# Projections of a transformer layer done as three bf16 products of split operands in place of fp32 products

## The reference

```python
def attn(x, Wq, Wkv_down, Wk_up, Wv_up, Wout):        # 16 heads of 64
    q = einsum('bld,dhk->blhk', x, Wq)
    latent = einsum('bld,dc->blc', x, Wkv_down)
    k = einsum('blc,chk->blhk', latent, Wk_up)
    v = einsum('blc,chk->blhk', latent, Wv_up)
    a = softmax(causal_mask(einsum('bqhd,bkhd->bhqk', q, k) / sqrt(64)))
    return einsum('bqhd,hdo->bqo', einsum('bhqk,bkhd->bqhd', a, v), Wout)

def ffn(x, Wg, bg, We, be):
    logits = x @ Wg + bg
    best_p = max over the 8 of softmax(logits)
    return (x @ We + be) * best_p[:, None]

x = x + layernorm(attn(layernorm(x), ...))
x = x + layernorm(ffn(layernorm(x), ...))
```

## Time and profile before

| | |
|---|---|
| time before, median of 2 runs | 2663.24 us (2646.28 to 2680.2) |
| the profiled execution | 2671.72 us |
| its span, slowest core (core 2) | 2670.2 us |
| spans of the eight cores | 2643.7 to 2670.2 us |
| TensorE matmul busy | 2046.2 us, 77% |
| ScalarE busy | 599.7 us, 22% |
| VectorE busy | 567.9 us, 21% |

### The profile page before, as it was taken

How to read it: one execution, slowest core, us unless ns; L and a number is a source line. 1 busy time by engine, 2 the same in 40 slices (tenths; PEclk the granted TensorE clock), 3 DMA queues, 4 the chain that set the end, 5 groups by cost and what they waited for, 6 DMA issues and landing times.

```text
span 2670.2 us, 18908 instructions; the slowest of 8 cores (2643.7 to 2670.2 us)
## 1 busy us (share of the span) xinstructions
PE 2046.2 (77%) x5377; PEld 786.7 (29%) x5377; DVE 567.9 (21%) x1050; ACT 599.7 (22%) x1372; POOL 75.4 (3%) x148
## 2 busy tenths in 40 slices
PE   5998987688696896877958769679699734458886
PEld 2444442122221222222222222122244322224443
DVE  2001001311312113122131121221000254323333
ACT  1111010044241442423414325134000111100000
POOL 0000000000000000000000000000000000000000
PEclk9777877799798897988979879789799866669998
DMA  3222210022121211211212212121200011002222
GB/s 91 71 71 79 63 49 27 4 9 8 8 8 8 8 6 8 10 9 11 14 12 16 16 26 16 10 11 14 32 16 24 17 40 47 24 16 95 89 93 71
DMA packets 101089, 83.31 MB, mean 31 GB/s; under 512 B 5248, under 2 KB 91776, under 8 KB 100992
## 3 DMA queue, kind: packets, MB, share of 16 engines
q0 software_dynamic: 11520, 37.76, 12.9%
q1 hardware_dynamic: 89472, 44.35, 6.0%
HBM read 61.12 MB, written 8.39 MB: 26 GB/s over the span
## 4 chain that ended last, share of the span: by engine, by line
PE 66%; DVE 12%; DMA 9%; issue 7%; ACT 5%; DVEq 1%; ACTq 0%; POOLq 0%; POOL 0%; SPq 0%
PE p L250 21%; PE p L488 14%; PE p L719 8%; PE p L432 8%; DMA PS<-SCR 7%; PE p L349 3%; PE p L363 2%; PE p L209 2%; DVE EB L478 1%; PE p L316 1%; ACT DSCR L472 1%; PE p L642 1%; ACT SCR L513 1%; ACT EB L458 1%; DVE EB L613 1%
## 5 line engine op out<-in xcount | busy, mean ns | idle before, releaser
L488 PE MATMUL p<-EB,VB 128*65 128x512 f32 (+3 forms) x1280 | 556.5, 553 | 120.6 <-DVE EB L478 102.3
L250 PE MATMUL p<-A,WS 128*128 128x512 f32 x1152 | 566.6, 661 | 28.8 <-DMA A<-PS 24.2
L250 PEld LDWEIGHTS p<-A,WS 128*128 128x128 f32 x1152 | 242.8, 211 | 349.6 <-issue 349.6
L432 PE MATMUL p<-B,KP 64*128 64x512 f32 (+3 forms) x640 | 319.7, 589 | 0.0
L437 PE MATMUL p<-B,KP 64*128 64x512 f32 (+3 forms) x640 | 319.6, 589 | 0.0
L458 ACT ACTIVATE EB<-p,NEGB 128x512 f32<-128x512 f32 x384 | 240.5, 685 | 255.7 <-PE p L437 255.1
L488 PEld LDWEIGHTS p<-EB,VB 128*65 128x65 f32 x1280 | 146.7, 139 | 482.2 <-issue 478.2
L719 PE MATMUL p<-B,WS 128*128 128x512 f32 x512 | 225.3, 603 | 0.0
L349 PE MATMUL p<-C,WU 128*128 128x512 f32 x256 | 128.6, 661 | 93.7 <-DVE KP L357 93.7
L432 PEld LDWEIGHTS p<-B,KP 64*128 64x128 f32 x640 | 101.0, 192 | 231.7 <-issue 231.7
L478 DVE TENSOR_TENSOR EB<-DSCR,TRI 128x128 f32<-128x128 f32 x256 | 74.7, 292 | 347.0 <-ACT DSCR L472 319.9
(11 more groups left out here) (92 smaller groups left out, 1069.3 us busy)
## 6 DMA issues: line engine op xcount, KB each, us to landing
XT<-x POOLq DMA_DIRECT2D x32, 512.0 KB, 3.9
WS<-wq SPq DMA_DIRECT2D x32, 512.0 KB, 4.5
WS<-we SPq DMA_DIRECT2D x32, 512.0 KB, 3.8
PS<-SCR POOLq DMA_DIRECT2D x64, 128.0 KB, 6.2
y<-XT POOLq DMA_DIRECT2D x16, 512.0 KB, 2.9
WS<-wkv SPq DMA_DIRECT2D x8, 512.0 KB, 4.4
A<-PS POOLq DMA_DIRECT2D x32, 128.0 KB, 2.2
WS<-wout SPq DMA_DIRECT2D x8, 512.0 KB, 3.9
```

What stands on the lines that cost most here:

```text
L250: r = o.matmul(ps[bank][:], WS[:, wslot * 1024 + kc * 128: wslot * 1024 + kc * 128 + 128], rhs_of(kc, nb), start=(kc == 0), stop=(kc == kc ...
L432: o.matmul(pA_[:, q0:512], KP[0:64, kc * 128:(kc + 1) * 128], B[0:64, p * 2048 + qb * 512 + q0: p * 2048 + (qb + 1) * 512], start=True, st ...
L488: return o.matmul(ps[pvbank][0:65, q0:512], VB[:, kc * 130 + sl * 65: kc * 130 + sl * 65 + 65], EB[:, eoff + q0:eoff + 512], start=(kc == ...
```

## The change

The products of `p2_part`, the output projection and the expert product are done in bf16. Each operand is written as hi + lo, where hi is its bf16 rounding and lo is the bf16 rounding of the rest, and each fp32 product becomes three bf16 products into the same PSUM bank: hi x hi, hi x lo and lo x hi. The up-projections, scores, value products, gate and transposes stay in fp32.

- **Weights** are split once (`wsplit`): load 128 columns over SP, ScalarE copies them to a bf16 hi, VectorE subtracts to a bf16 lo, and two DMAs on POOL's queue write both to internal DRAM tensors. The ten slices of wkv and wq are done at the very start, all landing in C under the one buffer `bC`. The slices of wout and we are done one each at the head of every pair of the attention, both landing in the same half of XT and both using the same half of the bf16 view of WS. All write-backs name one buffer, `bWH`.
- **Weights are read back** (`stream_b16`) by two DMAs of 256 KB each (128 runs of 2 KB) for every block of products, over SP.
- **Activations** are split before each 512-token stretch (`act_split`): eight ScalarE copies into AHI and eight VectorE subtractions into ALO. AHI lies over EB and ALO over VB; each exists once.
- **The output projection** has its loops turned: stretches outside, weight blocks inside, with 64 loads (32 pairs) in place of 8.
- The memset of VB is dropped, with its two columns of ones set after the q norms; the gate's weight goes to a tile of its own; `p6_b` normalizes through PS1 in place of EB.

```diff
+    AHI = nc.alloc_sbuf_tensor_at("AHI", [128, 4096], BF16, offset=nc.lookup_mloc(EB).addr)
+    ALO = nc.alloc_sbuf_tensor_at("ALO", [128, 4096], BF16, offset=nc.lookup_mloc(VB).addr)
+    WSB = nc.alloc_sbuf_tensor_at("WSB", [128, 4096], BF16, offset=nc.lookup_mloc(WS).addr)
+    bSTG = bEB + [bVB]
+    bWH = Buf("WHD")
-    s.op("vector", lambda o: o.memset(VB[:], 0.0), writes=[bVB])
+    def wsplit(dsrc, dhid, dlod, m, land, landbuf):
+        src = dsrc[:, m * 128:(m + 1) * 128].rearrange("(c p) n -> p c n",
+                                                       p=128)
+        landr = land.rearrange("p (c n) -> p c n", n=128)
+        s.op("sync", dma(landr, src), writes=[landbuf])
+        slot = m % 2
+        hi = WSB[:, slot * 2048:slot * 2048 + 1024]
+        lo = WSB[:, slot * 2048 + 1024:slot * 2048 + 2048]
+        s.op("scalar", lambda o, hi=hi, land=land: o.copy(hi, land),
+             reads=[landbuf], writes=[bWS[slot]])
+        s.op("vector", lambda o, hi=hi, lo=lo, land=land: o.tensor_sub(
+            lo, land, hi), reads=[landbuf, bWS[slot]], writes=[bWS[slot]])
+        s.op("gpsimd", dma(dhid[:, m * 1024:(m + 1) * 1024], hi),
+             reads=[bWS[slot]], writes=[bWH])
+        s.op("gpsimd", dma(dlod[:, m * 1024:(m + 1) * 1024], lo),
+             reads=[bWS[slot]], writes=[bWH])
+    for m in range(2):
+        wsplit(d_wkv, d_wkvh, d_wkvl, m, C[...], bC)
+    for m in range(8):
+        wsplit(d_wq, d_wqh, d_wql, m, C[...], bC)
...
+    def act_split(src_of, srcbufs, kchunks=8):
+        for kc in range(kchunks):
+            s.op("scalar", lambda o, kc=kc: o.copy(
+                AHI[:, kc * 512:(kc + 1) * 512], src_of(kc)),
+                reads=srcbufs, writes=[bSTG[kc % 5]])
+            s.op("vector", lambda o, kc=kc: o.tensor_sub(
+                ALO[:, kc * 512:(kc + 1) * 512], src_of(kc),
+                AHI[:, kc * 512:(kc + 1) * 512]),
+                reads=srcbufs + [bSTG[kc % 5]], writes=[bSTG[(kc + 1) % 5]])
+    def proj3(dst, dstbufs, wslot, kchunks, bank, scale=None, evac=None):
...
+                r = o.matmul(ps[bank][:], hw_, ha_, start=(kc == 0), stop=False)
+                r = o.matmul(ps[bank][:], hw_, la_, start=False, stop=False)
+                r = o.matmul(ps[bank][:], lw_, ha_, start=False,
+                             stop=(kc == kchunks - 1))
...
+        s.op("tensor", mmg, reads=[bWS[wslot]] + bSTG, writes=[bP[bank]])
+    def stream_b16(dhid, dlod, m, slot):
+        s.op("sync", dma(WSB[:, slot * 2048:slot * 2048 + 1024],
+                         dhid[:, m * 1024:(m + 1) * 1024]),
+             reads=[bWH], writes=[bWS[slot]])
+        s.op("sync", dma(WSB[:, slot * 2048 + 1024:slot * 2048 + 2048],
+                         dlod[:, m * 1024:(m + 1) * 1024]),
+             reads=[bWH], writes=[bWS[slot]])
     def p2_part(nb):
+        act_split(lambda kc, nb=nb: lnT_of(kc, nb), bAs[4 * nb:4 * nb + 4])
         for m in range(2):
...
+            stream_b16(d_wkvh, d_wkvl, m, slot)
+            proj3(C[...], [bC], slot, 8, 4 + m % 4)
...
     for p in range(8):
+        wsplit(d_wout, d_wouth, d_woutl, p, XT[... p % 2 ...], bXT[p % 2])
+        wsplit(d_we, d_weh, d_wel, p, XT[... p % 2 ...], bXT[p % 2])
         for wi, dsrc in enumerate((d_wku, d_wvu)):
...
+    for nb in range(4):
+        act_split(lambda kc, nb=nb: oT_of(kc, nb), list(bAs))
+        for m in range(8):
+            stream_b16(d_wouth, d_woutl, m, slot)
+            proj3(B[...], bBs[4 * nb:4 * nb + 4], slot, 8, (m + 2) % 4)
...
     for s4 in range(4):
+        act_split(lambda kc, s4=s4: ln3_of(kc, s4), bBs[4 * s4:4 * s4 + 4])
         for mf in range(8):
+            stream_b16(d_weh, d_wel, mf, slot)
...
+            proj3(None, None, slot, 8, bank, evac=ev)
```

More of the change, by code:

```diff
@@ L138, in build_nc @@
     DSCR = sb("DSCR", 256)
+    WGS = sb("WGS", 64)
     QN = KNS = DRS = LG = BPROW = SCR
+    AHI = nc.alloc_sbuf_tensor_at("AHI", [128, 4096], BF16,
+                                  offset=nc.lookup_mloc(EB).addr)
+    ALO = nc.alloc_sbuf_tensor_at("ALO", [128, 4096], BF16,
+                                  offset=nc.lookup_mloc(VB).addr)
+    WSB = nc.alloc_sbuf_tensor_at("WSB", [128, 4096], BF16,
+                                  offset=nc.lookup_mloc(WS).addr)
     ps = [es.enter_context(nc.psum_tensor(f"p{i}", [128, 512], F32))
@@ new lines, in proj3, with mmg @@
+    def proj3(dst, dstbufs, wslot, kchunks, bank, scale=None,
+              evac=None):
+        def mmg(o, wslot=wslot, kchunks=kchunks, bank=bank):
+            n = 0
+            for kc in range(kchunks):
+                hw_ = WSB[:, wslot * 2048 + kc * 128:
+                          wslot * 2048 + kc * 128 + 128]
+                lw_ = WSB[:, wslot * 2048 + 1024 + kc * 128:
+                          wslot * 2048 + 1024 + kc * 128 + 128]
+                ha_ = AHI[:, kc * 512:(kc + 1) * 512]
+                la_ = ALO[:, kc * 512:(kc + 1) * 512]
+                r = o.matmul(ps[bank][:], hw_, ha_, start=(kc == 0),
+                             stop=False)
+                r = o.matmul(ps[bank][:], hw_, la_, start=False, stop=False)
+                r = o.matmul(ps[bank][:], lw_, ha_, start=False,
+                             stop=(kc == kchunks - 1))
+            return r
+        s.op("tensor", mmg, reads=[bWS[wslot]] + bSTG, writes=[bP[bank]])
+        if evac is not None:
+            evac(bank)
+        elif scale is None:
+            s.op("scalar", lambda o, bank=bank: o.copy(
+                dst, ps[bank][:]), reads=[bP[bank]], writes=dstbufs)
+        else:
+            s.op("scalar", lambda o, bank=bank: o.activation(
+                dst, ps[bank][:], AF.Copy, scale=scale),
+                reads=[bP[bank]], writes=dstbufs)
@@ L290, in p2_part @@
+            proj3(C[:, m * 2048 + nb * 512:m * 2048 + nb * 512 + 512],
+                  [bC], slot, 8, 4 + m % 4)
         for m in range(8):
             slot = m % 2
[L292 to L301, removed]
+            stream_b16(d_wqh, d_wql, m, slot)
@@ L332, in build_nc @@
          reads=[bP[7]], writes=[bROWS])
+    s.op("vector", lambda o: o.memset(vb3[:, :, 64:65], 1.0), writes=[bVB])
+    s.op("vector", lambda o: o.memset(vb3[:, :, 129:130], 1.0), writes=[bVB])
     for p in range(8):
@@ L762, in p6_b @@
                      reads=[bP[bank], bMV[par]],
[L763 removed]
+                     writes=[bPS1h[par]])
             s.op("vector", lambda o, t=t, par=par: o.tensor_add(
                 XT[:, par * 1024:par * 1024 + 1024],
[L766 removed]
+                PS1[:, par * 1024:par * 1024 + 1024],
                 A[:, t * 1024:(t + 1) * 1024]),
[L768 removed]
+                reads=[bPS1h[par], bAs[t]],
                 writes=[bXT[par]])
```

89 lines of the change are left out of this document (36 added, 53 removed).

## The result

| | before | after |
|---|---|---|
| time, median of the runs measured together | 2698.5 us (2645.51 to 2862.76) | 2876.49 us (2864.46 to 3073.87) |
| ratio, 95% interval | | 1.0839 (1.0808 to 1.0871) |
| span of the profiled execution | 2670.2 us | 2866.4 us |
| granted TensorE clock, mean of a core | | 0.824 to 0.828, all eight |

The change makes the kernel 8.4% slower.

A forecast was written before the change was run, and what follows sets the result against it. TensorE products were taken to bound the kernel (busy 77%, 66% of the chain). 2671.7 - 185 (products) + 75 (start) + 163 (activation splits) + 105 (weight splits) = 2830, put at 2820 us; range 2740 to 2910 us.

The forecast's parts named there:

- A bf16 MATMUL of 0.2175 us: Projection and expert products: one bf16 MATMUL takes half an fp32 one, one cycle a column; 0.269 us at the lower clock.
- Rivals 4 and 5: Bf16 MATMULs of three stages: far under half an fp32 one, about 2555 us (0.04); as long, over 3250 us (0.03).
- The cold starts: TensorE restarts: 1 us each in the first projections, 6 us in the output projection, 5 us in the expert product.
- The saving of 185 us: Cheaper products: first projections -82 us, output projection -50, expert product -53.
- Read-back hidden: Between product blocks: a pair of 256 KB loads takes about 3.3 us, hidden under 5.2 us of products, at no cost.
- Rival 2: Between product blocks: a pair of loads takes 6.2 us, each of 64 blocks waits 1 us, 2885 us; chance 0.10.
- The start, +75: Kernel start: ten weight slices in a row at 6.8 us delay the first statistics to near 91.5 us, +75 us.
- Activation splits, +163: Ahead of twelve stretches: sixteen chained instructions of 12.3 us with TensorE idle, longer at three expert restarts; +163 us in all.
- Weight splits in the attention, +105: Head of each pair: splits delay the K up-projection, +14 us seven times and 7.5 us at pair 0; +105 us.
- Rival 3: Attention: the weight splits hide under the wait for the spreading DMAs, -95 us, 2725 us; chance 0.10.
- Rival 1: All product stages run at the lower clock, 0.269 us a MATMUL; later stages cost 40 us more, 2900 us; chance 0.13.
- the signals at its end: TensorE: twelve gaps of 12 to 17 us, busy time down near 185 us, share about 66%; first statistics near 91 us.

The follow-up runs named there:

- Either kernel with fp32 products: After with activation splits kept, no weight splits, fp32 products: 2799.53 us, ratio 1.0709; before with the weight splits added, fp32 products: 2830.31 us, ratio 1.0705.
- the kernel with all cures: After with weights split at first use, separate buffer names, piecewise first and last blocks, expert splits ahead of layer norm: 2550.6 us, ratio 0.9732.
- four one-edit variants: After with one edit each: hi/lo load names 1.0793; AHI/ALO piece names 1.0678; weight splits moved mid-pair 1.0538; start landing and write-back names 1.0958.
- the three edits together: After with separate names for hi/lo loads and for AHI/ALO pieces, and weight splits moved mid-pair: 2623.17 us, ratio 0.9938.

## Why the prediction was right or wrong

It said 2820 us, 5.9% slower, between 2740 and 2910. Direction and time hold; the loss was 8.4%, and 10.2% where before has the full clock, so the size of the change was put too low. Its steps:

**A bf16 MATMUL of 0.2175 us: right.** 0.216 us in every stage on every core of after. Rivals 4 and 5 fall. The Trainium skill (TensorE: Matmul & The Clock Gate, "Back-to-back issue gap") gives 131 ns as sustained and 216 ns as the isolated gap; this trace agrees with the second, in streams of 192 to 240.

**The cold starts: too small.** Behind the split's wait of 13.6 us the second stretch of core 7 has its first MATMULs 0.43 us apart for 5.8 us, with 0.50 granted, the lower of the two levels (1.2 GHz), then 0.216. The twelve starts there last 2.8 to 6.2 us and cost 1.3 to 3 us each, 28 us together, where the sum had 4 + 6 + 5 = 15.

**The saving of 185 us: 176 on the execution it was made against.** First projections 344 to 234 (-110, not -82), output projection 223 to 192 (-31, not -50), expert 225 to 189 (-36, not -53) on core 7 of after; waits for loads are in these sums. The larger first term was not better insight: the step carried core 2's lower clock of the earlier trace rows over to the changed kernel, and no profiled execution of the changed kernel has it. On core 1 of both kernels on the other chip the three are -51, -35 and -37.

**"Read-back hidden": wrong, and the largest miss.** 3.3 us for a pair was about right for two loads under way together (2.9 and 3.3 us each with the names apart). But the step read only sizes, and not that both DMAs write `bWS[slot]`, though the same working reckoned with that very rule for the two loads into WU. In a row they take over 5.5 us, more than a block's 5.2. Rival 2 had the wait, at 1 us in each of 64 blocks, but not its cause; it was about 0.6 us at each of the 92 boundaries between blocks (4 x 9 + 8 x 7), 52 us.

**The start, +75: right.** 73.6 us on the other chip, slices of 6.8 us, statistics at 90.74 us against 91.5.

**Activation splits, +163: 12.3 us right, the expert restarts too short.** The first product comes 12.3 us after the first copy. The three restarts of the expert stage have gaps of 32.2 to 32.7 us against 12.3 to 12.9 in before: +20, not +16.4. The step took the L764 at 2454.13 us for the last of its layer norm. It is the third of four; the same timeline of before goes on:

```profile
2456.97 1.23 DVE L764 TENSOR_TENSOR XT<-EB,A 128x1024 f32<-128x1024 f32 x1 [0.17 <-DVE EB L757]
```

3 us, three times, 9 us. In after the first subtraction stands directly behind the fourth:

```profile
2615.07 1.22 DVE L829 TENSOR_TENSOR XT<-PS,A 128x1024 f32<-128x1024 f32 x1 [0.17 <-DVE PS L822]
2616.21 0.69 DVE L322 TENSOR_TENSOR ALO<-B,AHI 128x512 bf16<-128x512 f32 x1
```

**Weight splits in the attention, +105: the order right, the size 137.** Of that 16.2 us at each of seven boundaries (14 predicted), 11 to 13 at pair 0 (7.5). Both have the same term short: a 128 KB load that starts right behind a 512 KB one landed after 4.8 us, not 2.2, as the page of after shows:

```profile
WU<-wku SPq DMA_DIRECT2D x8, 128.0 KB, 4.8
```

and the up-projection took 16.39 us, not 15.64. That leaves 12 us over the rest of the attention with no cause found. Either kernel with fp32 products shows about as much there, and the two amounts do not add. One thing goes with it: TensorE's busy time in the attention was 1094.39 us on core 7 and 1102.50 us on core 1 of the other chip, against 1088.18 in before, for the same 3097 or 3098 MATMULs, and the granted clock 0.84 and 0.83 against 0.88. About 3 us of this are the up-projections, already counted; whether the rest makes up the 12 us is not shown. Rival 3, the splits hidden, falls with the two timelines of the boundary.

**Rival 1, the lower clock everywhere: did not come;** no stretch of after is at it on any core. The Trainium skill (same page, "Part 1: The HAM clock gate") would budget 1.95 GHz for them: here about that is granted in some stretches of before and of the kernel with all cures, and in none of after, while 223 us of fp32 products on all cores had 0.99 of 2.4 GHz.

**Why the time was near and the change was not.** At full clock before is 2607 us; 2607 - 174 + 343 = 2776 us is what the forecast's own terms give there (174 being the saving with 71 for the first stage). Measured 2866 to 2874. The 90 to 98 us missing are the load waits 52, the attention 32, the fourth tile 9, and 6 in the products: 564 us without the load waits where these terms give 732 - 174 = 558, the longer cold starts in part made up by 0.216 for 0.2175 us. The forecast of 2820 stood on an execution with about 60 us of lowered clock in it, which the change took away; this hid part of the miss, and was luck. What the signals at its end named came: all twelve gaps, the busy time down (by 216), the share at 64%, not 66%; and of its three ways to be wrong, TensorE waiting for loads between blocks was the one that happened.

## What to carry over

When a change turns one transfer or one step into two, look first at the names by which the scheduler orders them: two halves under one name run in a row, and here two such names and one place in the list cost 246 us, more than the cheaper products gave (123 us on core 1 of the other chip, load waits included). Work put ahead of a wait pays for all that the wait was covering, its queued DMAs too; put the same work where the engine and the queue are idle. And make the sum against an execution whose clock is known to be the one that the changed kernel gets.

## What the hardware showed

- Three bf16 MATMULs cost 0.647 us where an fp32 product costs 0.859 (two of 0.4295): a quarter less, not more.
- Two 256 KB loads under way together on one queue land after 2.9 and 3.3 us, the pair in a row in over 5.5. Overlapping whole slices of the start gained less: each transfer grew (4.8 us), and the start shrank by 20 us.
- A product cut into eight pieces that each wait for the one before took 7.3 us for 24 MATMULs; undivided it took 5.2.
- The lower clock, 0.79 to 0.84 granted at 0.525 us per fp32 and 0.263 per bf16 MATMUL, fell on different cores, stages (the attention too) and chips with both data types. No stretch had it in the profiled executions of after (two), of its four one-edit variants and of the three edits together. What decides between a stretch that has it and one that hasn't is open.
